# Expert weights copied on GpSimd three at a time in the burst step, and the split of the biases one step later

## The reference: what is computed

```python
x = x + attn_a(layernorm(x))      # 16 heads of 8, biases, two masked corners
x = x + ffn(layernorm(x))
x = x + attn_b(layernorm(x))      # 16 heads of 8, scale sqrt(128)
x = x + ffn(layernorm(x))
# ffn, per item: gate = softmax(mean_tokens(x) @ gate_w.T); the best 2 of 8 experts, weights normed
# h = gelu(x @ down_w[e].T + down_b[e]);  out = sum_e w_e * (h @ up_w[e].T + up_b[e])
```

## Time and profile before

| | |
|---|---|
| median of 3 runs | 963.03 us |
| profiled execution | 963.5 us, span 961.7 us (1.8 us lie around the span) |
| busy | PE 859.7 us (89%), DVE 778.5 (81%), ACT 765.7 (80%), POOL 666.3 (69%) |
| mean granted clock of PE | 0.970 |
| chain that ended last | PE 53%, POOL 13%, DVE 11%, ACT 9%, issue 7%, DMA 3% |

### The profile page before, as it was taken

The page is one execution under the profiler, slowest core; times in us unless marked ns, Lnnn a source line. Parts: engine busy times, 40 slices in busy tenths (PEclk is TensorE's granted clock), DMA queues, the critical chain, the costliest instruction groups (busy, mean ns, idle before and its releaser), DMA issues.

```text
span 961.7 us, 33578 instructions
## 1 busy us (share of the span) xinstructions
PE 859.7 (89%) x13102; PEld 492.3 (51%) x13102; DVE 778.5 (81%) x1394; ACT 765.7 (80%) x1299; POOL 666.3 (69%) x1280
## 2 busy tenths in 40 slices
PE   2579999999999999999999999999999988988875
PEld 1235555555555555555555555555555544554543
DVE  1679999999998889888898989988878968869533
ACT  2168888888888888988888888988888877877863
POOL 8456777767886868868686877868777777654442
PEclk9689999999999999999999999999999999999986
DMA  6577555545544445435444454535445444344001
GB/s 184 156 216 221 156 158 172 159 140 157 157 154 126 127 145 143 146 111 151 135 146 136 137 154 126 147 122 157 125 125 165 120 139 127 109 133 135 4 24 45
DMA packets 144717, 132.04 MB, mean 137 GB/s; under 512 B 9616, under 2 KB 127536, under 8 KB 144432
## 3 DMA queue, kind: packets, MB, share of 16 engines
q1 hardware_dynamic: 143456, 128.49, 45.4%
q10 hardware_dynamic: 1104, 1.41, 0.5%
HBM read 73.76 MB, written 55.57 MB: 134 GB/s over the span
## 4 chain that ended last, share of the span: by engine, by line
PE 53%; POOL 13%; DVE 11%; ACT 9%; issue 7%; DMA 3%; SPq 1%; POOLq 1%; ACTq 1%; DVEq 0%
PE values_bank L779 16%; PE ring L808 9%; PE ring L794 8%; DVE nmax L601 8%; PE m_bank L907 5%; ACT probs L672 5%; PE ring L845 3%; PE m_bank L932 3%; PE m_bank L973 3%; POOL xy L492 2%; PE values_bank L920 2%; ACT hT L735 2%; POOL rest L508 1%; DMA q_stack<-maxT 1%; PE m_bank L946 1%
## 5 line engine op out<-in xcount | busy, mean ns | idle before, releaser
L601 DVE TENSOR_REDUCE nmax<-ring 128x4 f32<-128x1024 f32 x512 | 608.1, 1215 | 113.0 <-PE ring L794 109.5
L672 ACT ACTIVATE probs<-ring 128x1024 f32<-128x1024 f32 x512 | 512.1, 1026 | 92.3 <-PE ring L808 78.4
L779 PE MATMUL values_bank<-probs,values 128*32 128x256 f32 x4096 | 276.6, 384 | 0.7 <-ACT probs L672 0.7
L794 PE MATMUL ring<-k_stack,q_stack 64*128 64x256 bf16 x2048 | 191.4, 275 | 38.3 <-ACT probs L672 22.9
L492 POOL TENSOR_SCALAR xy<-x,mv,rstd 128x128 f32<-128x128 f32 x256 | 200.6, 793 | 7.9
L808 PE MATMUL ring<-q_stack,k_stack 64*128 64x256 bf16 x2048 | 180.1, 273 | 13.8 <-DVE nmax L601 8.2
L779 PEld LDWEIGHTS values_bank<-probs,values 128*32 128x32 f32 x4096 | 121.3, 109 | 61.4 <-issue 21.7
L808 PEld LDWEIGHTS ring<-q_stack,k_stack 64*128 64x128 bf16 x2048 | 78.0, 94 | 114.9 <-issue 54.7
L794 PEld LDWEIGHTS ring<-k_stack,q_stack 64*128 64x128 bf16 x2048 | 79.3, 95 | 111.0 <-ACT probs L672 42.4
L416 POOL TENSOR_SCALAR mparts<-nmax 128x32 bf16<-128x32 f32 x64 | 13.9, 217 | 164.8 <-DVE nmax L601 164.3
L508 POOL TENSOR_TENSOR rest<-qk,parts 128x512 f32<-128x512 f32 x64 | 74.2, 1159 | 5.4
(11 more groups left out here) (102 smaller groups left out, 1041.2 us busy)
## 6 DMA issues: line engine op xcount, KB each, us to landing
q_stack<-scratch SPq DMA_DIRECT2D x128, 256.0 KB
k_stack<-scratch SPq DMA_DIRECT2D x128, 256.0 KB
scratch<-parts SPq DMA_DIRECT2D x128, 192.0 KB, 2.2
scratch<-parts SPq DMA_DIRECT2D x128, 128.0 KB, 2.2
scratch<-parts SPq DMA_DIRECT2D x128, 64.0 KB, 2.4
out<-x SPq DMA_DIRECT2D x16, 256.0 KB, 2.6
x<-in_x SPq DMA_DIRECT2D x3, 768.0 KB, 6.7
q_stack<-maxT SPq DMA_DIRECT2D x128, 12.0 KB
```

The costliest lines, as they stand in the source:

```text
L601: nc.vector.tensor_reduce(dst, src, axis=AX.X, op=ALU.max, negate=True).then_inc(max_done, 1)
L672: nc.scalar.activation(probs[g % 2][:, c:c + 2, :, :], pair_of("exps", n, p)[:, :, :].rearrange("p x (k q) -> p x k q", k=TILES), ACT.Exp) ...
L779: last = nc.tensor.matmul(values_bank[32 * c:32 * (c + 1), a * TOKENS:(a + 1) * TOKENS], values[turn % RING][:, k, PER_GROUP * g + c, :], ...
L794: last = nc.tensor.matmul(pair_of("scores", turn, p)[:, a, t * TOKENS:(t + 1) * TOKENS], q_stack[z][rows, p, t * P:(t + 1) * P], k_stack[z ...
```

## The change

Two things are moved, both on POOL alone. First, of groups 1 to 9, 11 and 12 three turns are prepared in the burst step of the group before, and the fourth in the step behind it; before, the four turns stood in four successive steps (groups 1 to 7), or two and two in two steps. Unchanged are group 0, groups 10 and 13 (the first of batches 5 and 7) and the turns from 56 on. Second, `split_biases` moves from the end of step n (p = 7) to p = 1 of step n + 1, behind the split of the maxima.

```diff
+        def batch_of(turn):
+            return next(b for b, (first, rows) in enumerate(BATCHES) if first <= turn < first + rows)
+
         PREPARED = {}
         for group, burst in enumerate(BURSTS):
             for j in range(GROUP):
                 turn = group * GROUP + j
-                early_step = burst - (1 if turn >= LATE else GROUP - j if turn < ITEMS else 2 - j // 2)
+                before = BURSTS[group - 1] if group > 0 else None
+                if turn >= LATE:
+                    early_step = burst - 1
+                elif group == 0:
+                    early_step = burst - GROUP + j
+                elif batch_of(turn) in (5, 7) and turn == BATCHES[batch_of(turn)][0] // GROUP * GROUP + j:
+                    early_step = burst - 2 + j // 2
+                else:
+                    early_step = before if j < GROUP - 1 else before + 1
                 PREPARED.setdefault(early_step, []).append(turn)
...
                         split(src, tmp, hi, mid, lo, mhi_done, mrest_done, mmid_done, mparts_ready, n + 1)
+                    if p == 1 and batch_at(n, 4) is not None:
+                        split_biases(batch_at(n, 4))
...
                             nc.gpsimd.tensor_tensor(parts[i][:, 2], rest[i][:, :, :], parts[i][:, 1], ALU.subtract).then_inc(parts_ready, 1)
-                    if p == 7 and batch_at(n, 3) is not None:
-                        split_biases(batch_at(n, 3))
```

## The result

The changed kernel took **957.05 us** (median of six runs, 954.51 to 958.42; the kernel before 962.81 over six): ratio 0.9931, 95% interval 0.9904 to 0.9957. It is faster, and the time lies in the predicted range of 949.0 to 957.5, but at its upper end: the gain is 5.8 us where 11 were forecast. The profiled execution took 958.42 us, its span 956.6.

The account below looks back on a forecast made before the run. The prediction took the bound to be PE, reading in order, waiting at line 894 for POOL's late split maxima, nine times, 8.4 us. 963.5 - 7.8 - 3.2 - 1.0 + 1.2 - 0.5 = 952.2 us, range 949.0 to 957.5.

Parts of the forecast that it names:

- Late starts of POOL: Steps 21, 29, 37, 45, 48, 50, 53, 57: all eight PE stalls behind POOL at line 894 go, 7.8 us gained.
- Slow clock: Steps 54 and 58: without the stalls PE does not fall to its lower clock level, 3.2 us gained.
- Step 55: POOL 1.63 us earlier frees two of DVE's gate instructions, so PE waits 1.0 us less for DVE.
- Bursts with a choice: Steps 19, 27, 35, 43: later POOL parts make DVE's line 568 0.3 us late each, 1.2 us lost.
- POOL's idle time before the maxima: Sign that the forecast is right: in burst step 19 it falls from 6.63 to about 3.4 us.
- Transfers: Later parts in eleven burst steps cost zero; step 26's 0.52 us stall on the maxima's transfer goes, 0.5 us gained.
- The split behind the maxima: Normalization and parts of steps 14, 22, 30, 38, 46, 54, 58 come 2.12 us later; cost zero, up to 0.3 in step 14.
- rival D: Transfers of the eleven burst steps come late, about 0.8 us each, giving 961 us; chance 0.06.
- above 5 us in total: Sign for rival D: the total wait of PE's line 808 for the maxima's transfer exceeds this.
- rival B: Another wait refills half of the stalls in steps 54 and 58, with one slow stretch: 955.8 us; chance 0.20.
- Rival A: The slow clock stretch behind step 55's stall goes too, another 1.6 us, giving 950.6 us; chance 0.17.

Follow-up runs that it names:

- preps_only: Changed kernel with the split of the biases back at the end of the step, turns still prepared earlier; 959.97 us, ratio 0.9952 to the kernel before.
- split_only: Kernel before with only the split of the biases moved behind the next step's maxima, turns prepared as before; 963.39 us, ratio 0.9991.
- after_again: The changed kernel run once more, unaltered, for a second profile; 956.93 us, ratio 0.9938 to the kernel before.
- before_again: The kernel before, unaltered, one run for a second profile; 962.37 us.
- two_behind: two_in_best with step 55's one turn prepared behind the parts (p = 7 instead of p = 3); 955.09 us, ratio 0.9892 to the kernel before.
- two_in_best: Changed kernel with two turns instead of three prepared in bursts 19, 27, 35 and 43, the others in the two steps behind; 952.67 us, ratio 0.9894.
- one_input: Changed kernel with the gates' addition on DVE written with one SBUF input and the other as a per-partition scalar; 954.61 us, ratio 0.9917.
- four_in_best: Changed kernel with all four turns prepared in bursts 19, 27, 35 and 43, none in the step behind; 962.08 us, ratio 0.9989.

## Why the prediction was right, and where it was too large

The main mechanism was right; two sizes were off, by the terms' numbers:

1. *Late starts of POOL, −7.8:* −2.18 − 1.12 − 2.07 − 2.19 = −7.56 us by the step table. Right in size. By the same step lengths preps_only keeps 5.1 us of it, and split_only 2.5, as it gains 6.5 and loses 4.1 again in steps 22, 30, 38 and 46. "All eight stalls go" holds for the first profile only: with two preparations left in step 53, POOL is still 0.49 us late in step 54 of after_again. What is late next is DVE's maximum, as forecast (0.36 us in step 22).
2. *Slow clock, −3.2:* mis-sized. The step that failed is the one behind "without the stall PE has no reason to fall to the lower level": that the stall brings the fall, so that a fall seen once is booked as its price. Before_again has the stalls, 2.25 and 2.32 us, without the fall. The 3.2 us were those of one execution, and other executions fall elsewhere (a longer stretch in burst 56 in before_again, steps 12 and 60 in the changed kernels). The mean granted clock of the runs of one set shows no gain: 0.974 over 21 runs of the kernel before and 0.974 over the ten of after_again, where two stretches of 3.4 us less would raise it by about 0.0035 (an estimate, 2 x 3.4 x 0.5 / 961); the runs of one kernel scatter by 0.004.
3. *Step 55, −1.0:* −0.93. Right; two_behind took another 0.85 us of that wait away (2.37 to 1.52).
4. *Bursts with a choice, +1.2:* mis-sized. POOL's parts ended just where computed: at 304.24, which is 0.48 us behind the moment at which line 576 would have started without the hold (304.47 − 0.71); 0.50 was computed. But the list of DVE's instructions to be held began at line 568; the addition two instructions earlier was left out; in step 55 it had escaped by 0.04 us. It is held 0.7 us in each burst: 2.20 for bursts 19, 35 and 43, and the same 0.72 in burst 27 (there hidden in part by term 5), 2.9 in all. Two_in_best and one_input show it. POOL's idle time before the maxima is 4.09 us instead of the 3.4 foretold, because the maxima come 0.7 us later.
5. *Transfers, −0.5:* the stall of 0.52 at 398.23 is gone, and burst 27 grew by only 0.29 instead of 0.73. Whether POOL's earlier end in step 25 removed it is not shown: split_only still prepares a turn there and has no such stall (burst 27 17.84 us). The 3.26 us by which the parts end later hold for seven of the eleven burst steps; 47, 49, 54 and 56 had two turns before and end 1.63 later. PE's wait for the maxima's transfers is 7.2 us in two places, 4.6 of it the opening and 2.5 the stall of step 54, which comes and goes. So the sign given for D, "above 5 us in total", came true by its letter, but it was ill chosen, as the kernel before had 5.5 already. No burst step but the four with a choice of experts is longer in after_again than before by more than 0.1 us, so rival D did not happen.
6. *The split behind the maxima:* zero, since step 14 kept its 12.21 us in both profiles.

Without the second term the measured ones give 962.81 − 7.56 − 0.93 + 2.20 + 0.29 = 956.8 us, beside 957.05 measured. The middle of the forecast was 4.8 us too low, 3.2 of it term 2 and 1.8 terms 4 and 5. The prediction had given 0.62 to 953.4 us and less and 0.36 to what came, a gain within 1%; that the range held the time is in part luck, as its upper end was reckoned for rival B. B's picture, a wait on the maxima's transfer in step 54, stood in the profile taken, but not in its repeat. Rival A (the clock of step 55 holds) came in neither profile of the changed kernel, with a stall of 2.37 us left; it is seen once, in two_behind, behind a stall of 1.52.

## What to carry to other kernels

Before work of POOL is moved beside VectorE, list every instruction of VectorE in the new stretch, the tiny ones too, and ask of each whether it has two inputs in SBUF or several elements in a partition, as those that were held in these runs had; a row that shows it short at another moment does not clear it. Moving work into another engine's idle time has a dose: two turns in these bursts cost nothing, three 0.73 us, four 1.5. And a slow-clock stretch seen in one profile is a cost of that execution until a second profile shows it at the same place.

## What the runs showed of the hardware

- The same stall is followed by the lower clock in one execution and not in another. With 1.36 us in step 11, the kernel before stayed at 1.00 and the kernel after fell to 0.51. Stalls of 2.25 to 2.51 us went without a fall (before_again, and step 54 of the kernel after), one of 1.98 us with it (four_in_best). The rows of PE and the window behind, of the kernel before:

```profile
200.31 0.39 PE L808 MATMUL ring<-q_stack,k_stack 64*128 64x256 bf16 x4 [1.36 <-DVE nmax L601]
...
200.50:203.90 3.40, 3.40 (x73) 2.19 (x69) 2.45 (x3) 2.36 (x5) 1.80 (x6) 1.00 0.23 65
```

and of the kernel after, whose window from 201.1 stands above:

```profile
200.77 0.39 PE L816 MATMUL ring<-q_stack,k_stack 64*128 64x256 bf16 x4 [1.36 <-DVE nmax L609]
```

- An instruction of VectorE on eight numbers (8 partitions, one element each) can take 0.86 us instead of 0.15, because of what POOL does at that moment (two_in_best: 0.15 with POOL's part out of the way); POOL's tensor_scalar held VectorE as its tensor_tensor did (line 523 in four_in_best, 0.50 instead of 0.22 us for the multiply).
